# A gated attention block on one core: queries turned by a transposing DMA from tile 9 on, the epsilon of the layer norms on VectorE, a new order at the start

## The reference, cut to what matters

```python
q = layernorm(x)                        # 16 heads of 16 numbers
scores = einsum('bhqd,bhkd->bhqk', q, ctx) / 4
attn = softmax(where(causal, scores, MIN))
x = x + tanh(g_xattn) * (attn @ ctx)    # keys and values are both ctx
xn = layernorm(x)
prob = softmax(xn @ w_router + b_router)        # 16 blocks of 64 hidden units
mask = the 4 blocks of highest prob, for each row
h = relu(xn @ w1.T + b1) * mask                 # 1024 hidden units
x = x + tanh(g_ffn) * (h @ w2.T + b2)
```

## Time and profile before

| | |
|---|---|
| median of 3 runs | 728.71 us (727.47 to 730.14) |
| the profiled execution | 730.76 us |
| its span | 728.8 us |
| PE busy | 695.8 us, 95% |
| POOL, DVE, ACT busy | 524.1, 505.8, 474.1 us |
| share of PE in the chain that ended last | 92% |
| granted TensorE clock, mean of the span | 0.988 |

### The profile page before, as it was taken

One profiled execution on the slowest core, in us unless ns is written; L12 is line 12 of the kernel. 1 busy time (PEld: TensorE's weight loads), 2 busy tenths in 40 slices (PEclk: granted clock), 3 DMA queues, 4 the chain that ended last, 5 costly groups with the idle time before them and its releaser, 6 DMA issues.

```text
span 728.8 us, 30742 instructions
## 1 busy us (share of the span) xinstructions
PE 695.8 (95%) x13284; PEld 646.7 (89%) x13284; DVE 505.8 (69%) x1428; ACT 474.1 (65%) x780; POOL 524.1 (72%) x725
## 2 busy tenths in 40 slices
PE   5668999999999999999999999999999999999988
PEld 4557899999999999999999999999999999998887
DVE  5366877667767766776776677678677767865552
ACT  2465766766776676677667667766766676676432
POOL 6577878777877877787777778777777877775542
PEclk9798999999999999999999999999999999999999
DMA  4312232333243233324324332432332233210010
GB/s 153 90 33 65 64 80 50 79 76 44 72 78 79 50 80 76 54 61 79 79 53 78 75 58 57 79 79 57 74 75 64 52 79 80 30 42 20 17 37 29
DMA packets 101589, 46.95 MB, mean 64 GB/s; under 512 B 75472, under 2 KB 101200, under 8 KB 101456
## 3 DMA queue, kind: packets, MB, share of 16 engines
q1 hardware_dynamic: 101184, 43.95, 27.5%
q10 hardware_dynamic: 272, 1.05, 0.5%
...
## 4 chain that ended last, share of the span: by engine, by line
PE 92%; ACT 3%; DMA 2%; DVE 1%; POOL 1%; issue 1%; SPq 1%; POOLq 0%; ACTq 0%
PE score_banks L310 10%; PE score_banks L283 9%; PE bank L390 8%; PE bank L411 8%; PE bank L413 8%; PE bank L323 8%; PE bank L412 8%; PE bank L392 8%; PE bank L391 8%; PE bank L250 5%; PE bank L338 4%; PE bank L349 3%; PE score_banks L293 1%; PE bank L362 1%; ACT weights L470 1%; DMA qT<-qT 1%
## 5 line engine op out<-in xcount | busy, mean ns | idle before, releaser
L724 POOL TENSOR_SCALAR_AFFINE_SELECT weights<-weights 128x1024 f32<-128x1024 f32 x128 | 137.7, 1099 | 126.9 <-ACT weights L470 126.8
L731 POOL TENSOR_TENSOR h_low<-hid,h_high 128x512 fp32r<-128x512 f32 x128 | 166.5, 1301 | 39.3 <-ACT hid L492 38.9
L621 DVE SCALAR_TENSOR_TENSOR hid<-bank,b_cols,used_all 128x256 f32<-128x256 f32 x248 | 108.1, 477 | 75.9 <-PE bank L392 73.3
L390 PE MATMUL bank<-xT_high,w_high 128*128 128x256 f32 x496 | 150.2, 303 | 0.0
L470 ACT ACTIVATE weights<-score_banks 128x1024 f32<-128x1024 f32 x128 | 124.3, 1023 | 39.4 <-PE score_banks L310 39.4
L411 PE MATMUL bank<-w_high,h_high 128*128 128x256 f32 x488 | 137.6, 282 | 3.2 <-DVE y_out L606 2.6
L392 PE MATMUL bank<-xT_high,w_low 128*128 128x256 f32 x496 | 140.2, 283 | 0.0
L391 PE MATMUL bank<-xT_low,w_high 128*128 128x256 f32 x496 | 139.6, 281 | 0.0
L413 PE MATMUL bank<-w_high,h_low 128*128 128x256 f32 x488 | 138.1, 283 | 0.0
L412 PE MATMUL bank<-w_low,h_high 128*128 128x256 f32 x488 | 137.7, 282 | 0.0
L411 PEld LDWEIGHTS bank<-w_high,h_high 128*128 128x128 f32 x488 | 92.1, 189 | 3.8 <-DVE y_out L606 3.0
...
## 6 DMA issues: line engine op xcount, KB each, us to landing
...
qT<-qT SPq DMA_DIRECT2D x128, 4.0 KB
...
kT_parts<-k_parts SPq DMA_TRANSPOSE x57, 3.1
used_all<-used SPq DMA_TRANSPOSE x32, 2.6
```

Source lines behind the costliest of these rows:

```text
L390: pe.matmul(out=bank, lhsT=w1_high[:, k, c], rhs=high, start=k == 0, stop=False)
L621: dve.scalar_tensor_tensor(hid[:, n % 4, j], hid_bank(n)[:, j * TOKS:(j + 1) * TOKS], b1_cols[:, c:c + 1], used_all[:, p % 2], ALU.add, AL ...
L724: pool.affine_select(out=w, in_=w, compare_op=ALU.is_ge, fill=0.0, base=0, pattern=[[0, 2 * HB], [1, S]], channel_multiplier=-1).then_inc( ...
L731: pool.tensor_tensor(h_low[:, p % 2, chunks], hid[:, n % 4], h_high[:, p % 2, chunks].bitcast(F32), ALU.subtract).then_inc(h_low_made, 1)
```

## The change

Queries go the way of the keys from tile 9 on (`QUERIES_BY_PE`), with the maxima: DVE writes the maxima to `max_found_in` and copies their halves into `q_parts` (`maximum_parts`), POOL splits the queries (`query_parts`), SP issues a second transposing DMA for each tile ahead of that for the keys, and ACT joins the halves (`q_joined`), now behind the first hidden parts of an iteration. For that the queries are normalised one iteration earlier. The epsilon of both layer norms is added by DVE, behind the statistics. The early queries and keys are turned into the banks of the FFN, and from iteration 0 on ahead of the scores. At the start PE makes 16 transposes of the identity whose result nothing reads, the first tile is loaded by itself, the context by ACT's queue; ACT makes the mask's tiles and loads its table ahead; five of the eight low parts of the weights go from POOL to DVE.

Numbers and PE's list:

```diff
+WARM = 16
...
+        QUERIES_BY_PE = OUT_LAG + 2
+
+        def q_early(b):
+            return b < QUERIES_BY_PE
+
+        def k_early(b):
+            return b < KEYS_BY_PE
...
         def pieces_of(i):
-            n = {-1: 0, 0: 2, 2: 4, 3: 6}.get(i, 8)
-            return range(n, n + 2) if n < 8 else ()
+            return {0: (0, 1), 1: (2, 3), 2: (4, 5), 3: (6,), 4: (7,)}.get(i, ())
+
+
+        W_LOW_BY_POOL = (0, 2, 4)
...
                 for r in range(HB):
-                    turned = pe.transpose(banks[M1][:, r * S:(r + 1) * S],
+                    turned = pe.transpose(banks[OUT_BANK][:, r * S:(r + 1) * S],
...
             pe.wait_ge(ident_made, 1)
+            for n in range(WARM):
+                pe.transpose(banks[M0][:, 0:P], ident[:], ident[:])
             for i in ITERATIONS:
                 pr, pu = router_pair(i), used_pair(i)
                 p, m = hidden_pair(i)
                 out_b = out_tile(i)
-                if i + 1 == 0:
-                    pe.wait_ge(mask_made, 2 * U)
-                if 0 <= i + 1 < N:
-                    scores(i + 1)
-                if 0 <= i + 2 < N + MAX_LAG:
-                    q_transposed(i + 2)
-                if 0 <= i + 2 < KEYS_BY_PE:
-                    k_transposed(i + 2)
+                if i < 0:
+                    if i + 1 == 0:
+                        scores(0)
+                    if i + 2 >= 0:
+                        k_transposed(i + 2)
+                        q_transposed(i + 2)
+                else:
+                    if q_early(i + 2):
+                        q_transposed(i + 2)
+                    if k_early(i + 2):
+                        k_transposed(i + 2)
+                    if i + 1 < N:
+                        scores(i + 1)
                 if p is not None:
                     hidden(p, m)
```

ACT:

```diff
+
+            def q_joined(b):
+                n, slot = divmod(b - QUERIES_BY_PE, 2)
+                act.wait_ge(q_spread[slot], 16 * (n + 1))
+                act.copy(qT[:, b % TS, :].bitcast(U16).rearrange("p (n h) -> p h n", h=2),
+                         qT_parts[:, slot]).then_inc(q_copied, 1)
...
+            act.dma_start(c_in[:, 0, :], A_ctx[0]).then_inc(c_first_landed, 16)
+            act.dma_start(c_in[:, 1:PAIR, :], A_ctx[1:PAIR].rearrange("b p d -> p b d")).then_inc(c_landed[0], 16)
+            act.dma_start(c_in[:, PAIR:2 * PAIR, :], A_ctx[PAIR:2 * PAIR].rearrange("b p d -> p b d")).then_inc(c_landed[1], 16)
+
+            act.wait_ge(numbers_set, 2)
+            act.activation(scratch[:], half_power[:], ACT.Exp)
+            act.wait_ge(triangle_made, 1)
+            for u in range(U):
+                rows = slice(u * PAD, (u + 1) * PAD)
...
             for i in ITERATIONS:
                 pr, pu = router_pair(i), used_pair(i)
                 p, m = hidden_pair(i)
-                if 0 <= i + 2 < N + MAX_LAG:
+                if i < 0 <= i + 2:
+                    k_evacuated(i + 2)
                     q_evacuated(i + 2)
-                if 0 <= i + 2 < KEYS_BY_PE:
-                    k_evacuated(i + 2)
-                elif KEYS_BY_PE <= i + 2 < N:
-                    k_joined(i + 2)
+                elif i >= 0:
+                    if q_early(i + 2):
+                        q_evacuated(i + 2)
+                    if k_early(i + 2):
+                        k_evacuated(i + 2)
+                    elif i + 2 < N:
...
                     exponentials(i)
                 if p is not None:
                     hidden_parts(p, m)
+                if QUERIES_BY_PE <= i + 3 < N + MAX_LAG:
+                    q_joined(i + 3)
                 if pr is not None:
                     choice(pr)
                 if 0 <= i - 2 < N:
                     x_copies(i - 2)
```

DVE:

```diff
+            def stats_of(source, stats, mv, ve, s, b, stats_made, mean_made, ve_made):
                 dve.bn_stats(stats[:, s, :], source).then_inc(stats_made, 1)
                 dve.wait_ge(stats_made, b + 1)
                 dve.bn_aggr(mv[:, s, :], stats[:, s, :]).then_inc(mean_made, 1)
+                dve.wait_ge(mean_made, b + 1)
+                dve.tensor_scalar(ve[:, s], mv[:, s, 1:2], LN_EPS, None, ALU.add).then_inc(ve_made, 1)
...
+                if QUERIES_BY_PE <= b - QS:
+                    dve.wait_ge(q_parts_made, b - QS - QUERIES_BY_PE + 1)
+                elif b >= QS:
+                    dve.wait_ge(q_turned, b - QS + 1)
                 dve.tensor_scalar(q_pad[:, b % QS, :, 0:HD], x_in[:, b % XS, :].rearrange("p (h d) -> p h d", d=HD),
                                   mv1[:, s, 0:1], rstd1[:, s], ALU.subtract, ALU.mult).then_inc(qn_made, 1)
 
             def row_maximum(b):
                 dve.wait_ge(scored, b + 1)
-                ride = q_pad[:, (b + MAX_LAG) % QS, :, RIDE_COL].rearrange("p (t g u) -> p u t g", g=2, u=U)
+                carrier = b + MAX_LAG
+                ride = q_pad[:, carrier % QS, :, RIDE_COL] if q_early(carrier) else max_found_in[:]
+                ride = ride.rearrange("p (t g u) -> p u t g", g=2, u=U)
                 found_in = score_banks[:, :, 0:2 * WIDTH].rearrange("p u (t k) -> p u t k", k=WIDTH)
                 dve.tensor_reduce(out=ride[:, :, :, 1], in_=found_in[:, :, :, HALF:WIDTH],
                                   axis=AX_X, op=ALU.max, negate=True)
                 dve.tensor_reduce(out=ride[:, :, :, 0], in_=found_in[:, :, :, 0:HALF],
                                   axis=AX_X, op=ALU.max, negate=True).then_inc(max_found, 1)
+
+            def maximum_parts(b):
+                carrier = b + MAX_LAG
+                n, slot = divmod(carrier - QUERIES_BY_PE, 2)
+                dve.wait_ge(max_found, b + 1)
+                if n == 0:
+                    dve.wait_ge(q_parts_ready, LEVELS)
+                else:
+                    dve.wait_ge(q_spread[slot], 16 * n)
+                dve.tensor_copy(q_parts[:, slot, :, :, RIDE_COL],
+                                max_found_in[:].bitcast(U16).rearrange("p (h l) -> p l h", l=2)).then_inc(max_parts_made, 1)
 
             def attention_added(b):
...
                 if 0 <= i + 1 < N:
                     row_maximum(i + 1)
+                    if not q_early(i + 1 + MAX_LAG):
+                        maximum_parts(i + 1)
                 if 0 <= i - 2 < N:
                     normalised_again(i - 2)
                 if 0 <= i + 4 < N:
                     layernorm_stats(i + 4)
                 if p is not None:
                     hidden_masked(p, m)
-                if 0 <= i + 3 < N:
-                    normalised(i + 3)
...
+                    places(0)
+                    places(1)
                 if 0 <= i - 3 < N:
                     x_parts(i - 3)
                 if pr is not None:
                     route(pr)
+                if 0 <= i + 4 < N:
+                    normalised(i + 4)
+                if i == FIRST + 1:
+                    places(2)
+                    places(3)
                 if p is not None:
                     hidden_masked(p, m + 1)
+                weights_low(i)
```

POOL and SP:

```diff
-            def rstd_of(mv, ve, result, s, b, mean_made, ve_made, rstd_made):
-                pool.wait_ge(mean_made, b + 1)
-                pool.tensor_scalar(ve[:, s], mv[:, s, 1:2], LN_EPS, None, ALU.add).then_inc(ve_made, 1)
+            def rstd_of(ve, result, s, b, ve_made, rstd_made):
                 pool.wait_ge(ve_made, b + 1)
                 pool.tensor_tensor(result[:, s], ve[:, s], half_power[:], ALU.pow).then_inc(rstd_made, 1)
...
+            def query_parts(b):
+                n, slot = divmod(b - QUERIES_BY_PE, 2)
+                pool.wait_ge(qn_made, b + 1)
+                if n >= 1:
+                    pool.wait_ge(q_spread[slot], 16 * n)
+                pool.tensor_copy(q_parts[:, slot, :, :, 0:HD],
+                                 q_pad[:, b % QS, :, 0:HD].bitcast(U16).rearrange("p h (d l) -> p l h d", l=2)
+                                 ).then_inc(q_parts_made, 1)
...
+                if QUERIES_BY_PE <= i + 3 < N:
+                    query_parts(i + 3)
                 if KEYS_BY_PE <= i + 3 < N:
                     key_parts(i + 3)
...
+                    pool.memset(q_parts[:, :, :, :, HD:], 0).then_inc(q_parts_zeroed, 1)
+                    pool.wait_ge(q_parts_zeroed, 1)
+                    for n in range(LEVELS):
+                        pool.memset(q_parts[0:(n + 1) * PAD, :, 1, :, LEVEL_COL + n:LEVEL_COL + n + 1], NEG_HIGH
+                                    ).then_inc(q_parts_ready, 1)
...
+            def queries_spread(b):
+                slot = (b - QUERIES_BY_PE) % 2
+                if b - 2 >= QUERIES_BY_PE:
+                    sync.wait_ge(q_copied, b - 1)
+                if b < N:
+                    sync.wait_ge(q_parts_made, b - QUERIES_BY_PE + 1)
+                sync.wait_ge(max_parts_made, b - QUERIES_BY_PE + 1)
+                sync.dma_start_transpose(qT_parts[:, slot].rearrange("p l (r s) -> p (l r) s", s=S),
```

(9 more changed lines are left out.)

130 lines of the change are left out of this document (76 added, 54 removed).

## The result

| | before | after |
|---|---|---|
| median of 4 runs each, same chip | 729.18 us (727.47 to 730.14) | 722.93 us (721.73 to 724.09) |
| ratio after to before | | 0.9917, 95% interval 0.989 to 0.9943 |
| the profiled execution, its span | 730.76, 728.8 us | 723.54, 721.8 us |
| PE, DVE, ACT, POOL busy | 695.8, 505.8, 474.1, 524.1 | 686.2, 576.3, 514.2, 512.2 |
| share of PE and of DVE in the chain that ended last | PE 92% | PE 61%, DVE 24% |

The account below looks back on a forecast made before the run. PE, busy throughout the steady window, was taken to bound the kernel. 730.76 - 23.4 + 8.7 - 7 = 709.1 for a profiled execution, less 2.05 for the median: 707 us; eight-in-ten range 694 to 730.

Parts of the forecast that it names:

- The transposes: On PE: the query transposes are gone 57 times at 0.41 us each, all on the path, -23.4 us.
- What DVE gets: On DVE: two epsilon adds (0.17 each) and one copy of maxima (0.20) fit the slack before `y_out` and `hid`, 0 us.
- What ACT and POOL get: ACT's join delays POOL's second `h_low` by 1.25; `xn` meets `x_b`, PE waits 0.31 in about 28 iterations without router, +8.7 us.
- The transposing DMA: Queries' DMA through SP's queue lands at 321.5, ACT wants it at 321.7: slack 0.2, thin, 0 us.
- The start: First tiles: shorter rounds, early loads and earlier clock rise, less added memsets, together -7 us, ends -4 and -13.
- -1.5 (first load, table): At the start: first tile loaded by itself and table loaded ahead of first use, -1.5 us, an estimate without a row.
- +1.3 (memsets): At the start: more memsets on POOL, a second set for `k_parts`, ahead of the first router, +1.3 us.
- Both kinds of iteration pay: Epsilon add over about 0.19, or query normalisation meets POOL: wait grows 0.2 to 0.35 per iteration; 717, up to 727; 22%.
- The epsilon waits for POOL: DVE's small add is held up by POOL's split, 0.34 in each iteration: 726, or 731 with `y_out`'s slack used; 8%.
- The spread comes late: At `q_joined` on ACT: queries' DMA lands at 4.2, ACT 0.9 late in 28 iterations without router, +25, so 732; 8%.

## Why the prediction was wrong, step by step

**The transposes (-23.4).** The term was right on PE: the first product of `hidden` now stands 0.27 behind the last scores, where the transposes stood. In iterations with router 0.30 of the 0.41 arrived.

**What DVE gets: this step failed.** "By itself this costs nothing, and nothing is left over" rested on 0.17 for an add, with 0.20 for the copy. The adds took 0.15, but 0.19 to 0.22 with their waits, and the copy 0.24 to 0.76. The runs that leave them out put the price at 0.35 us a pair, 9.3 us over the 26.5 pairs of tiles 9 to 62 (between these tiles the trace without them is shorter by 560.35 - 552.28 = 8.1; the rest is within the scatter of the pair). The forecast had this term at 0. The prediction had the mechanism in its hands: it let `xn` be held up by `x_b` and the copy, another DVE instruction between SBUF tiles that stands right ahead of `xn`, pass in 0.20. A slack of 0.01 was taken for enough. At `y_out` the forecast left 0.10 and no time for the handover, which it did count for `hid` (0.06). In the trace `y_out` ends 0.09 ahead of PE's start (414.93 and 415.02), with router 0.06, and PE's next start comes late: 0.23 behind instead of 0.12, here with router:

```profile
404.51 0.39 PE L437 MATMUL bank<-w_high,h_high 128*128 128x256 f32 x1
404.74 0.28 PE L438 MATMUL bank<-w_low,h_high 128*128 128x256 f32 x1
```

**What ACT and POOL get (+8.7).** `h_low` came 1.26 later, as forecast, and with nothing added on DVE a pair takes 20.82, 0.43 above the floor of 20.39, where 0.31 was forecast. That the size is so near is in part luck. By PE's starts, in the run with neither copy nor adds, the wait for `hid` is 0.21 without router and 0.06 with it, and 0.18 is a wait that the forecast did not have: the shifted scores, 1.19 behind the attention instead of 1.01, wait for the rows of maxima, as they never did before. On SP the two small DMAs that move these rows stand behind `used_spread`, a transposing DMA that waits for ACT's `used`. By the join that one now goes out 1.25 later in the row, and the small ones right behind it. SP before, then after:

```profile
312.11 1.17 SPq L841 DMA_TRANSPOSE used_all<-used  x1
314.91 1.16 SPq L812 DMA_DIRECT2D qT<-qT  x2
```

```profile
413.26 1.96 SPq L961 DMA_TRANSPOSE used_all<-used  x1
415.27 1.16 SPq L921 DMA_DIRECT2D qT<-qT  x2
```

Before, SP was through with it at 313.28, 1.6 ahead of the small DMAs; now at 415.22, at their start. With the join behind the hidden parts `used_spread` is as early as it was, and the wait is gone in every iteration. How it comes about is not shown to the end: in some iterations the shifted scores wait though the small DMAs went out as early as 2.07 behind the start of DVE's row, so the landing is late too, and no run changes SP's order alone.

**The transposing DMA (0).** Landing 3.3, not 3.1, and slack used up 13 times. No run isolates its price. The figure of 1309 ns a block in the Trainium skill (VectorE: DVE Perf Modes, "The three transpose paths") would by the prediction's estimate have doubled the time; the 3.3 us for eight blocks exclude it once more.

**The start (-7).** First scores came at 8.54 (forecast 8.3). No run shows the terms -1.5 (first load, table) and +1.3 (memsets) by themselves. The rounds, from one shifted scores to the next in the timeline of PE, were 7.0 and 6.8, about as forecast (6.9), and then 8.0:

```profile
18.45 1.17 PE L335 MATMUL score_banks<-qT,kT 32*128 32x128 f32 x32 [2.06 <-DVE q_pad L640]
...
25.48 1.17 PE L335 MATMUL score_banks<-qT,kT 32*128 32x128 f32 x32
...
32.26 1.17 PE L335 MATMUL score_banks<-qT,kT 32*128 32x128 f32 x32 [1.04 <-DVE q_pad L640]
...
40.23 2.09 PE L335 MATMUL score_banks<-qT,kT 32*128 32x128 f32 x32 [2.32 <-DVE q_pad L640]
```

Up to there the start had gained what was forecast: these shifted scores of tile 3 stood at 47.08 before and stand at 40.23 now, 6.9 earlier. By tile 9 it is 4.3. Later rounds lose to POOL part of what the order gains: `x` behind the mask, and `xn` behind the memsets and then behind three POOL instructions in a row (DVE, then POOL). One of the low parts of the weights that DVE was given is held up too, 1.58 at 34.67 beside the mask against 0.68 at 42.25.

```profile
44.47 1.42 DVE L666 SCALAR_TENSOR_TENSOR x<-att,tanh_g,x_in 128x256 f32<-128x256 f32 x1
...
49.03 1.70 DVE L674 TENSOR_SCALAR xn<-x,mv,rstd 128x256 f32<-128x256 f32 x1 [0.54 <-POOL rstd L793]
```

```profile
48.97 0.72 POOL L868 TENSOR_TENSOR x_b<-x,gated_b 128x256 f32<-128x256 f32 x1
49.64 0.39 POOL L801 COPY v_pad<-c_in 128x256 f32<-128x256 f32 x1
49.98 0.60 POOL L808 COPY k_parts<-c_in 128x512 uint16<-128x512 uint16 x1
```

**The rivals.** "Both kinds of iteration pay" (717, up to 727) is the nearest: its time holds the result, and its condition, an add over about 0.19, was met. But of its two iterations mostly the one without router pays: 10.64 against 10.39 - 0.41, 0.66 of loss, and with router 10.52 against 10.82 - 0.41, 0.11. "The epsilon waits for POOL" named the right cause and the wrong instruction: the one-column add is never held up, the copy is. "The spread comes late" was there as waits of ACT and had no price that could be shown.

The sum, corrected: 709.1, plus 9.3 for what was added on DVE, 3.2 for the 0.12 a pair beyond the forecast (26.5 pairs) and 2.7 that the start did not give, less 0.8 at the end: 723.5; the profiled execution took 723.54. The terms are differences of these same traces, so that they add up is bookkeeping and no second proof; what the runs show by themselves is the 0.35 a pair for what was added on DVE. The start's 2.7 and the end's 0.8 are no larger than what profiles of kernels with nearly the same program there differ by, 4 and 1.5.
